# Where GpSimd gathers rows in the expert stage of a decoder layer: after each output scatter, or grouped in the middle of every wide expert

## What is computed

```python
def _L0_ffn_ref(inputs, gate_kernel, w0, w1, wo):
    NUM_EXPERTS, TOP_K = 64, 2
    x = inputs.reshape(b * s, e)                      # 4096 tokens of 256
    gate_logits = jnp.einsum('te,ex->tx', x, gate_kernel)
    weights, selected = jax.lax.top_k(gate_logits, TOP_K)
    weights = jax.nn.softmax(weights.astype(jnp.float32), axis=-1)
    ...
    h0 = jax.lax.ragged_dot(sorted_x, w0, group_sizes)
    h1 = jax.lax.ragged_dot(sorted_x, w1, group_sizes)
    inter = jax.nn.silu(h0) * h1
    out_sorted = jax.lax.ragged_dot(inter, wo, group_sizes)
    ...
x = x + _L0_attn_ref(_layernorm(x), ...)
x = x + _L0_xattn_ref(ctx_1024, _layernorm(x))
x = x + _L0_ffn_ref(_layernorm(x), ...)
```

## Time and profile before

| | us |
|---|---|
| median of 3 runs | 1365.47 |
| lowest and highest | 1364.45 and 1366.08 |
| span of the profiled execution | 1362.8 |

### The profile page before, as it was taken

The page is one execution under the profiler, slowest core; times in us unless marked ns, Lnnn a source line. Parts: engine busy times, 40 slices in busy tenths (PEclk is TensorE's granted clock), DMA queues, the critical chain, the costliest instruction groups (busy, mean ns, idle before and its releaser), DMA issues. The chain is left out here.

```text
span 1362.8 us, 20764 instructions
## 1 busy us (share of the span) xinstructions
PE 1039.0 (76%) x6769; PEld 921.1 (68%) x6769; DVE 904.0 (66%) x2041; ACT 574.8 (42%) x1282; POOL 649.3 (48%) x591
## 2 busy tenths in 40 slices
PE   4767878778787775776567764699999999999940
PEld 3656767767676774665215653699999888888840
DVE  6999999999999984887986664233232232323218
ACT  3768787787878653443404441121121212111100
POOL 4887888878788832000003555334434344434310
PEclk8999999999999997555778796799999999999985
DMA  8544646465555622123030111788778788888629
GB/s 238 194 137 134 182 146 188 152 186 166 169 172 157 183 59 57 31 43 51 33 123 32 40 40 32 259 275 268 267 259 268 268 274 272 274 271 269 238 75 348
DMA packets 163531, 232.62 MB, mean 171 GB/s; under 512 B 34380, under 2 KB 87996, under 8 KB 162656
## 3 DMA queue, kind: packets, MB, share of 16 engines
q1 hardware_dynamic: 145808, 207.79, 48.7%
q0 software_dynamic: 11280, 19.06, 4.2%
q10 hardware_dynamic: 6336, 4.44, 1.0%
HBM read 203.08 MB, written 23.95 MB: 167 GB/s over the span
## 5 line engine op out<-in xcount | busy, mean ns | idle before, releaser
L1011 PE MATMUL st_y_ps<-ident,st_hc 128*128 128x128 f32 x2048 | 274.0, 292 | 113.9 <-DVE st_hc L530 113.9
L1011 PEld LDWEIGHTS st_y_ps<-ident,st_hc 128*128 128x128 f32 x2048 | 255.5, 203 | 136.5 <-DVE st_hc L530 135.6
L413 POOL TENSOR_TENSOR st_u<-st_dx,codes 128x1024 f32<-128x1024 f32 x127 | 296.5, 2360 | 40.9 <-DVE st_h L522 31.9
L522 DVE TENSOR_TENSOR_SCAN st_h<-st_da,st_u 128x512 f32<-128x512 f32 x256 | 297.7, 1204 | 0.8 <-ACT st_da L749 0.8
L2203 PE MATMUL mo_h<-mo_xt,w 128*128 128x128 f32 (+17 forms) x2048 | 281.1, 288 | 1.9 <-DVE mo_xt L2300 1.9
L2203 PEld LDWEIGHTS mo_h<-mo_xt,w 128*128 128x128 f32 x2048 | 270.4, 192 | 6.7 <-issue 2.7
L2306 DVE TENSOR_TENSOR mo_inter<-mo_silu,mo_h 128x128 f32<-128x128 f32 (+17 forms) x256 | 75.7, 304 | 281.2 <-ACT mo_silu L2277 217.1
L2144 POOL DMA_INDIRECT outs<-mo_o,choice x95 | 93.7, 986 | 232.6 <-DVE mo_o L2317 219.4
L2277 ACT ACTIVATE mo_silu<-mo_h 128x128 f32<-128x128 f32 (+17 forms) x256 | 71.7, 290 | 311.8 <-PE mo_h L2203 210.9
L749 ACT ACTIVATE st_da<-st_delta,st_a_neg 128x510 f32<-128x510 f32 x256 | 171.7, 685 | 57.2 <-DVE st_h L522 52.8
L530 DVE TENSOR_TENSOR st_hc<-st_h,st_cps 128x1024 f32<-128x1024 f32 x128 | 152.7, 1193 | 0.0
(11 more groups left out here) (359 smaller groups left out, 1416.4 us busy)
## 6 DMA issues: line engine op xcount, KB each, us to landing
codes<-bc SPq DMA_DIRECT2D x256, 256.0 KB, 3.8
w<-in_L_ffn_w_dram SPq DMA_DIRECT2D x128, 512.0 KB
wo<-in_L_ffn_wo_dram SPq DMA_DIRECT2D x64, 512.0 KB
co_got<-outs SPq DMA_DIRECT2D x16, 512.0 KB, 6.0
wave<-dist SPq DMA_DIRECT2D x16, 274.0 KB
x<-in_x_dram SPq DMA_DIRECT2D x8, 512.0 KB, 9.2
st_cx<-in_ctx_dram SPq DMA_DIRECT2D x8, 512.0 KB, 4.1
dist<-st_dd SPq DMA_DIRECT2D x32, 128.0 KB, 3.6
```

The lines of the kernel that those rows point to most:

```text
L413: nc.gpsimd.tensor_tensor(u_sb[k % URING][:, :, :], dx[p % 2][:, :, :], over_chunks(b_sb[k % BRING]), ALU.mult).then_inc(u_ok, 1)
L522: nc.vector.tensor_tensor_scan(h_sb[k % HRING][:, dh, :], da_ps[dh][:, :], u_sb[k % URING][:, dh, :], 0.0, ALU.mult, ALU.add).then_inc(h_o ...
L1011: m = nc.tensor.matmul(y_ps[t // 2][:, t % 2, dh * P:(dh + 1) * P], hc_sb[k % RING][:, dh, t * P:(t + 1) * P], K.ident[:, :], start=False, ...
```

## The change

The gathers no longer stand between the scatters. When a wide expert k comes up, POOL waits for its third product (`inter_ok` at 4k + 3), then gathers for experts k + 3 and k + 4, one transfer and two, and scatters k. For a narrow expert it only scatters. The start gathers experts 1 and 2 ahead, no longer 3. The gather for the late loop, with its small copy, moves into a function and from k = 59 to the third product of expert 60. The set of transfers is the same, and the scatters keep their own order.

```diff
-            for k in range(1, XR):
+            def gather_late():
+                nc.gpsimd.tensor_copy(to[:, :], K.choice[:, LATE0:LATE0 + 1]).then_inc(indices, 1)
+                pool.wait_ge(turned, RANKS - XR + 1)
+                nc.gpsimd.indirect_dma_start(xg[LAST][:, 0, :], None, K.xn_dram[:, :],
+                                             bass.IndirectOffsetOnAxis(ap=K.table[:, LATE0:LATE0 + 1], axis=0)
+                                             ).then_inc(x_in[LAST], 16)
+
+            for k in range(1, XR - 1):
                 gather(k)
             for k in range(RANKS):
-                if k + XR < RANKS:
-                    gather(k + XR)
-                if k + XR == RANKS:
-                    nc.gpsimd.tensor_copy(to[:, :], K.choice[:, LATE0:LATE0 + 1]).then_inc(indices, 1)
-                    pool.wait_ge(turned, RANKS - XR + 1)
-                    nc.gpsimd.indirect_dma_start(xg[LAST][:, 0, :], None, K.xn_dram[:, :],
-                                                 bass.IndirectOffsetOnAxis(ap=K.table[:, LATE0:LATE0 + 1], axis=0)
-                                                 ).then_inc(x_in[LAST], 16)
+                if wide[k]:
+                    pool.wait_ge(inter_ok, k * FC + 3)
+                    for j in (k + XR - 1, k + XR):
+                        if j < RANKS:
+                            gather(j)
+                        if j == RANKS:
+                            gather_late()
                 scatter(k)
```

## The result

| | before | after |
|---|---|---|
| median | 1364.96 us (4 runs, 1362.88 to 1366.08) | 1341.52 us (4 runs, 1340.06 to 1342.29) |
| span of the profiled execution | 1362.8 us | 1340.0 us |

The ratio is 0.9829, with a 95% interval of 0.9815 to 0.9843: 23.4 us less, on the chip of the profile of before. As the experiments show further down, another chip gives 1315 us for both kernels, so this ratio is one of a chip and not of the kernel alone.

The account below looks back on a forecast made before the run. PE was taken to bound the expert stage, only its idle time being winnable. Span 1362.8 - 25.4 = 1337.4, all other terms 0; median 2.7 above, 1340.1; half a microsecond more, 1340.6 us; range 1338 to 1354.

Parts of the forecast that it names:

- What bounds the stage: Expert stage: PE sets the pace, working 323.91 of 341 us, and never waits on a weight load.
- The line: Stall-free length of a wide expert: 5.70 + 0.04 x (columns - 134) us; 155.6 us for 24 wide experts.
- The cause: Wide experts: a long unbroken run of indirect DMAs on POOL holds back PE's done signals; 25.4 us over 24 experts.
- Three gathers late in the wide expert: Gathers starting 3.82 us into each wide expert, the third near the next narrow one: 0 taken, at most 7.5 us lost.
- Rival A: The third transfer of a run still holds a little: gain only 17.9 us, 1347.6 us; chance 0.18.
- Gathers later, scatters earlier, bandwidth: Expert stage: later gathers, earlier narrow-expert scatters and less transfer time, 291 in place of 270 GB/s, each cost 0.
- The end and the start: First gathers moved into expert 0, late gather and copy moved to expert 60's third product: 0 each.
- The 0.5 us for odds and ends: Half a microsecond added to the forecast time for odds and ends of hold that remain.
- The gain: Wide experts 10 to 58 without 36: breaking the run of six takes 181.0 us to 155.6, 25.4 us less.
- Rival B: Only part of the hold goes, perhaps half stays, if the amount POOL sends in a stretch counts: 1352.8 us; chance 0.11.
- Rival C: No change, 1365.5 us: POOL's run and late silus only coincide, the reason lying in the wide expert itself; chance 0.09.
- Rival D: Slower, 1389.6 us: transfers beside a wide expert's PE work hold, now hitting up 3, down 1 and the transposes; chance 0.07.

Follow-up runs that it names:

- mixed kernels: Changed kernel with POOL's order set per wide expert by a table: 1315.95 us on chip 2; with waits in routing too, 1372.12 on chip 7, 1353.19 on chip 5.
- order M: In some pairs of the mixed kernels, all six transfers unbroken behind the wide expert's third product, against the changed kernel: 1372.12 us for the whole kernel on chip 7.

## Why the prediction was right

**What bounds the stage: right.** With the stalls gone PE works all of 320 us, and it waits for neither weights nor gathers.

**The line: right to 0.02 us** of 155.60, on each chip, in every expert that isn't held. Two experts free of stalls (8 and 60) were enough to price all the others.

**The cause: right, and it need not have been.** The prediction took it from two neighbouring experts, one without the end of the six and one place in routing, and coincidence could have done as much. The mixed kernels bear it out on chips that hold: six in a row hold wherever they are put, and three with 1.7 us of pause before the next three lose nothing. What it calls runs of three without harm in every narrow expert are the first three of the six, which start before the harm. In one point it was lucky. It took a pause "of over a microsecond" for enough; 1.07 us left 0.83 us on chip 7. The order that was made has 1.9 us and more on either side of the three gathers. Between the second and the third scatter it has only 1.1 to 1.6 us, once 0.45, and there it didn't matter, since even without that pause the run is three.

**Three gathers late in the wide expert: right, at 0.** The hold that they still make is there, up to 1.2 us on a silu of the narrow expert, and falls into the slack that the prediction named. Rival A, a third of a run still holds, had the effect right and its price wrong.

**Gathers later, scatters earlier, bandwidth: right, at 0.** PE never waits on a gather in the timeline, at 291 GB/s for 320 us. The last pairs, which the prediction set against a possible ceiling of 300, ran at 311 GB/s (experts 56 and 57) with PE busy throughout.

**The end and the start: 0 forecast, 2.76 us measured**, 1.63 of it the clock of the late expert. The prediction asked only who waits for whom there, and not at which clock the same rows would run. The 0.5 us for odds and ends stood for something else, and took up little of it. The gain was 25.65 in place of 25.4: experts 36 and 37 gave back their 0.25 as well. Span: 1337.9 forecast with the half microsecond, 1340.0 measured; the median, 1341.52 to 1340.6, comes closer since it lay 1.5 us above the profiled span in place of 2.7.

**Rival B, only a part goes**: on the first chip wrong, and four, five and six in a row with the same transfers in the same stretch speak against it on chip 5. **Rival C, no change**: wrong on the first chip, and right on chip 4 (0.9998), for a reason that the prediction never considered, that there was nothing to remove. The Trainium skill's sentence ("SBUF — State Buffer", section "Who interferes with whom") that PE and ACT never wait on anyone stands among rules on shared SBUF ports, and no run here shows that the hold has to do with ports. Read more widely, as a rule for timing, it fits chips 2 and 4, and the measurement decides against it on the four others. There PE's rows start at their usual pace in a hold, but who waits for PE starts up to 3.7 us late on chip 12 and 4.1 on chip 7, in order M. The ends of PE's rows are modelled in the profile, so whether the results were there and only the signal was late isn't shown. **Rival D**, a hold that moves to the transposes: not seen in the changed kernel. It exists, as the 0.83 us of expert 40 on chip 7 shows, and the 0.25 us around expert 36, from which rival A was priced, belong to it too, with DVE told of the transposes 0.5 us late. M shows that the hold can be moved at a price of 1.9 to 2.8 us for each pair.

**What the prediction lacked** is the chip. Its numbers hold for the chip of the profile alone; on chips 12, 7 and 5 the changed kernel as a whole was never run. The chances for faster should have been read as chances on a chip that holds.

## What to carry to other kernels

Look for places where a signal of PE comes late with nobody busy, and lay them beside POOL's row of indirect DMAs: runs of three with pauses of 1.7 us between cost nothing here, four up to 0.7 us, and five or six 0.7 to 2.4 us of PE each time, once PE's slack is used up, and up to 3.6 us on chip 12, where the clock fell behind the longest holds. Where an expert is slow and nobody was late, look at its granted clock before you look for a wait. Price a stall by the same work elsewhere in the trace that has none, as a line over its size. And before a gain in such waiting is believed, time both kernels on a second chip: a trace shows the chip as well as the kernel.

## What the runs showed of the hardware that was not expected

- The same kernel takes 1315, 1365 or 1380 us, by the chip, each within about 0.3% over its runs. All fourteen traces reach routing's first indirect transfer at 738.5 to 741.0 us, holding chips at 739.2 to 741.0, so it is no general slowness. Four of six chips held, if the first, whose number isn't on record, is none of the others. Whether it belongs to the chip, to its place in the machine or to a state that lasts, these runs don't tell, and nor do they by what path POOL's transfers reach PE's signals.
- Held signals often come in bunches: two or three silus run one right behind the other, 1.0 to 1.2 us behind the end of the run's last transfer (1197.90 behind 1196.89; 1211.66 behind 1210.48). It isn't always so. In expert 38 of the kernel before the silu of part 1 starts at 1139.06, while the sixth transfer still runs, and the other two at 1140.54, 1.3 us behind its end.
- On chips that held, a large part of the profile's records of semaphore updates is missing from routing on (311 of 1024 present for routing's transfers on the first chip, 1023 on chip 4). A trace in which landing times are blank is a mark of such a chip here.
- A hold can bring the clock down: PE idles in it, and then 3.4 us at the lower level follow, which cost 0.79 us in an expert that had no hold of its own. It happened six times between experts 10 and 60, four on chip 12 and two on chip 7, and never on the first chip or chip 5.
- Shorter gathers don't help: with at most 32 rows in each gather the loss was 0.76 to 2.35 us on chip 7, no less than with 128.
- An unbroken row of 64 indirect transfers over 81 us held nothing on chips 2 and 4.
- The clock of the late expert fell to a granted 0.70 in the changed kernel (5.46 us for 32 rows), and stood at 1.00 in the kernel before (3.83 us), behind the same idle times of PE. It isn't a matter of one execution: both traces of the kernel before, on the first chip and chip 12, have 3.83 us, and the twelve others, on chips that held and chips that didn't, have 5.27 to 5.46. What decides it is open.
